# Head-by-head exponential of the query softmax on ScalarE, and a ring of four PSUM banks for the query and value products

## The reference

```python
qkv = jnp.einsum('bnc,cf->bnf', x, w_qkv)
q, k, v = jnp.split(qkv, 3, axis=-1)          # each reshaped to B, N, 8 heads, 64
q = jax.nn.softmax(q, axis=-1)                # over the 64 columns of a head
k = jax.nn.softmax(k, axis=1)                 # over the 1250 nodes
context = jnp.einsum('bnhd,bnhe->bhde', k, v / N)
out = jnp.einsum('bhde,bnhd->bhen', context, q / sqrt(64))
```

## Time and profile before

| | |
|---|---|
| median of 3 runs | 558.52 us (558.47 to 559.47) |
| the profiled execution | 561.2 us |
| its span, first to last instruction | 558.6 us, granted clock 0.954 |
| busy: PE, DVE, ACT, POOL | 496.5, 342.3, 233.5, 165.5 us |
| the changed stage | 105.6 to 182.9 us of the span |

### The profile page before, as it was taken

The page is one execution under the profiler, slowest core; times in us unless marked ns, Lnnn a source line. Parts: engine busy times, 40 slices in busy tenths (PEclk is TensorE's granted clock), DMA queues, the critical chain, the costliest instruction groups (busy, mean ns, idle before and its releaser), DMA issues.

```text
span 558.6 us, 11588 instructions
## 1 busy us (share of the span) xinstructions
PE 496.5 (89%) x3909; PEld 389.9 (70%) x3909; DVE 342.3 (61%) x731; ACT 233.5 (42%) x533; POOL 165.5 (30%) x142
## 2 busy tenths in 40 slices
PE   2988599999889889999999988799999978989792
PEld 2776488766455756679988877599888857856541
DVE  4679888589798267555266543212675375537686
ACT  4744122553323422224255448211355377733343
POOL 1564400040860300024974610000446023304312
PEclk9998799999999899999999997899999957999997
DMA  8502200020200200020000010000210294000014
GB/s 247 164 2 75 76 1 3 1 75 1 77 0 1 78 1 1 1 79 0 0 1 0 11 66 1 3 1 0 82 48 0 79 412 191 2 0 2 0 54 129
DMA packets 5246, 27.45 MB, mean 49 GB/s; under 512 B 1036, under 2 KB 1161, under 8 KB 3544
## 3 DMA queue, kind: packets, MB, share of 16 engines
q1 hardware_dynamic: 5208, 26.92, 13.9%
HBM read 24.36 MB, written 2.56 MB: 48 GB/s over the span
## 4 chain that ended last, share of the span: by engine, by line
PE 65%; DVE 19%; ACT 7%; issue 5%; POOL 1%; DVEq 1%; DMA 1%; ACTq 0%; SPq 0%
PE ps L455 38%; PE ps L600 15%; PE ps L442 4%; PE ps L509 3%; PE ps L499 2%; DVE stage L1447 2%; DVE ohs L1078 1%; DVE r L1159 1%; DVE r L1087 1%; DVE late L1088 1%; PE ps L709 1%; PE ps L439 1%; ACT r L920 1%; DVE r L1517 1%; ACT late L837 1%
## 5 line engine op out<-in xcount | busy, mean ns | idle before, releaser
L455 PE MATMUL ps<-late,wslot 128*128 x960 | 104.7, 269 | 1.0 <-ACT ohs L894 0.9
L455 PE MATMUL ps<-r,wslot 128*128 128x250 f16 x840 | 99.8, 279 | 5.1 <-DVE r L1087 5.0
L455 PEld LDWEIGHTS ps<-late,wslot 128*128 128x128 f16 x960 | 92.3, 97 | 13.1 <-issue 3.5
L1578 POOL TENSOR_TENSOR wslot<-stage,wslot 128x2048 f16<-128x2048 f32 x9 | 36.8, 4086 | 206.4 <-ACT wslot L752 129.0
L455 PEld LDWEIGHTS ps<-r,wslot 128*128 128x128 f16 x840 | 84.3, 101 | 18.5 <-DVE r L1087 6.6
L600 PE MATMUL ps<-late,r 125*128 (+1 forms) x800 | 90.5, 274 | 4.9 <-issue 3.4
L600 PEld LDWEIGHTS ps<-late,r 125*128 125x128 f16 x800 | 78.6, 99 | 15.1 <-issue 6.0
L455 PE MATMUL ps<-wslot,r 128*125 128x512 f16 x300 | 71.3, 387 | 2.6 <-DVE late L1088 2.6
L1088 DVE SCALAR_TENSOR_TENSOR late<-ps,late 128x250 f32 (+2 forms) x60 | 29.1, 502 | 61.2 <-ACT late L927 55.6
L455 PEld LDWEIGHTS ps<-wslot,r 128*125 128x125 f16 (+1 forms) x300 | 39.5, 138 | 26.5 <-DVE late L1088 4.0
L759 ACT ACTIVATE late<-ps 125x500 f16<-125x500 f32 (+1 forms) x25 | 14.7, 588 | 100.6 <-PE ps L442 100.6
(11 more groups left out here) (174 smaller groups left out, 697.2 us busy)
## 6 DMA issues: line engine op xcount, KB each, us to landing
late<-in_tv SPq DMA_DIRECT2D x2, 4096.0 KB, 17.4
x<-in_x SPq DMA_DIRECT2D x5, 448.0 KB
out<-r SPq DMA_DIRECT2D x10, 224.0 KB
stage<-in_w_up SPq DMA_DIRECT2D x2, 1024.0 KB, 5.1
stage<-in_w_down SPq DMA_DIRECT2D x2, 1024.0 KB, 4.9
stage<-in_w_lin SPq DMA_DIRECT2D x1, 1024.0 KB, 6.8
stage<-in_w_k SPq DMA_DIRECT2D x1, 1024.0 KB, 6.1
stage<-in_w_q SPq DMA_DIRECT2D x1, 1024.0 KB, 4.7
```

The lines of the kernel that those rows point to most:

```text
L455: last = nc.tensor.matmul(out, stat_(hs, b), mov(hm, b), start=start and n == 0, stop=stop and n == 3 * blocks - 1)
L1578: nc.gpsimd.tensor_tensor(wslot[:, i % SLOTS, 1].rearrange("p k n -> p (k n)"), stage[:, :], wslot[:, i % SLOTS, 0].rearrange("p k n -> p ...
```

## The change

Three things change in the QV stage. The q and v products get a family of their own, "z", with a ring of four banks (0 to 3) in place of two. The subtraction on VectorE is dropped: VectorE now makes the negated maximum of each head and scales that small tile (125x8), and ScalarE reads the product from PSUM in eight exponentials of 64 columns, each with its own bias column and an accumulated sum, so that the sum reduction on VectorE is dropped too. The bank of a q tile is freed by the last of those exponentials, not by VectorE's subtraction. Nothing of the order of tiles changes.

```diff
-    "n": [("qv", 2 * T, "dve", 0), ("m", KB, "dve", 1), ("mix", T, "dve", 0), ("ffn2", T, "dve", 0)],
+    "z": [("qv", 2 * T, "dve", 0)],
+    "n": [("m", KB, "dve", 1), ("mix", T, "dve", 0), ("ffn2", T, "dve", 0)],
...
-RING = {"n": 2, "t": 4, "x": 2, "y": 2}
+RING = {"z": 4, "n": 2, "t": 4, "x": 2, "y": 2}
...
+            def qv_tile(i):
+                kind, t = QV[i]
+                if i < RING["z"]:
+                    wait_done(pe, "t", "k", 17 + i)
+                else:
+                    last_kind, last_t = QV[i - RING["z"]]
+                    pe.wait_ge(q_exp if last_kind == "q" else v_low, last_t + 1)
+                passes(bank("z", i % RING["z"])[0:P, :], lambda h, b: xn_t[:, h, b, t * P:(t + 1) * P],
+                       lambda h, b: weight(kind)[:, h, b, :], KB).then_inc(full["z"], 1)
...
-                    wait_done(act, "n", "qv", i + 1)
-                    nc.scalar.activation(q_nat[:, t, :], q_nat[:, t, :], ACT.Exp, scale=S_XW).then_inc(q_exp, 1)
+                    act.wait_ge(q_minus, t + 1)
+                    for h in range(H):
+                        part = slice(h * DH, (h + 1) * DH)
+                        last = nc.scalar.activation(q_nat[:, t, part], bank("z", i % 4)[0:P, part], ACT.Exp, scale=S_XW,
+                                                    bias=qmax[:, t, h:h + 1], accum_out=qsum[:, t, h:h + 1])
+                    last.then_inc(q_exp, 1)
...
-                then(nc.vector.tensor_reduce(qmax[:, t, :], q, AX.X, ALU.max))
-                nc.vector.tensor_tensor(heads_of(q_nat[:, t, :]), q, per_head(qmax[:, t, :]), ALU.subtract).then_inc(free["n", "dve"], 1)
+                nc.vector.tensor_reduce(qmax[:, t, :], bank("z", i % 4)[0:P, :].rearrange("p (h d) -> p h d", h=H), AX.X, ALU.max,
+                                        negate=True).then_inc(q_max, 1)
+                dve.wait_ge(q_max, t + 1)
+                nc.vector.tensor_scalar(qmax[:, t, :], qmax[:, t, :], S_XW, None, ALU.mult).then_inc(q_minus, 1)
 
             def q_sum(t):
                 dve.wait_ge(q_exp, t + 1)
-                then(nc.vector.tensor_reduce(qsum[:, t, :], heads_of(q_nat[:, t, :]), AX.X, ALU.add))
                 nc.vector.reciprocal(qsum[:, t, :], qsum[:, t, :]).then_inc(q_rec, 1)
```

More of the change, by code:

```diff
@@ L99 @@
 }
-RING = {"n": 2, "t": 4, "x": 2, "y": 2}
-BANKS_FROM = {"qv": ("t", "k", 17), "agg0": ("n", "mix", 9), "ffn2": ("t", "ffn1", 9)}
+RING = {"z": 4, "n": 2, "t": 4, "x": 2, "y": 2}
+BANKS_FROM = {"agg0": ("n", "mix", 9), "ffn2": ("t", "ffn1", 9)}
 def before(family, phase, who=None, high=False):
@@ L146 @@
 assert sum(WINDOWS.values()) * J == NWIN and J == HT
-READER = {"lin": ("t", "lin"), "k": ("t", "k"), "q": ("n", "qv"), "v": ("n", "qv"), "out": ("n", "m"), "up0": ("t", "up0"),
+READER = {"lin": ("t", "lin"), "k": ("t", "k"), "q": ("z", "qv"), "v": ("z", "qv"), "out": ("n", "m"), "up0": ("t", "up0"),
           "down0": ("t", "down0"), "up1": ("t", "up1"), "down1": ("t", "down1"), "gate": ("t", "gate")}
@@ L168, in bank @@
                 return ps[:, slot, 0:CH]
-            return ps[:, {"n": 0, "x": 4, "y": 6}[family] + slot, :]
+            return ps[:, {"z": 0, "n": 0, "x": 4, "y": 6}[family] + slot, :]
         x = sb("x", [P, T, D])
@@ L475, in transposed, with natural_tile @@
                     product_chunk(phase, w, mov, j, bass.ts(j, CH))
[L477 to L480, removed]
+            def natural_tile(phase, mov, w, t):
+                wait_bank(pe, "n", phase, t, t % 2)
+                passes(bank("n", t % 2)[0:P, :], lambda h, b: mov[:, h, b, t * P:(t + 1) * P], lambda h, b: w[:, h, b, :], KB
                        ).then_inc(full["n"], 1)
+            def qv_tile(i):
[7 more added lines that the diff above has]
+                       lambda h, b: weight(kind)[:, h, b, :], KB).then_inc(full["z"], 1)
             def natural(phase, mov, w, blocks=KB, ready=None, bias=None):
@@ L548, in _ @@
                     wait_weight(pe, "v")
-                natural_tile("qv", xn_t, weight(kind), t, i)
+                qv_tile(i)
                 if kind == "q" and KN_LAG <= t < Q_FIRST:
@@ L556, in _ @@
             windows("v", HT - 1, 1, 2)
-            wait_done(pe, "n", "qv", 2 * T)
+            pe.wait_ge(q_exp, T)
+            pe.wait_ge(v_low, T)
             wait_done(pe, "x", "kn", T)
@@ L845, in _ @@
                             high_tile_nat("x", "kn", k_nat, S_K, u, u % 2)
-                    wait_done(act, "n", "qv", i + 1)
-                    nc.scalar.activation(q_nat[:, t, :], q_nat[:, t, :], ACT.Exp, scale=S_XW).then_inc(q_exp, 1)
-                else:
-                    wait_full(act, "n", "qv", i)
-                    nc.scalar.activation(v_nat[:, 0, t, :], bank("n", i % 2)[0:P, :], ACT.Copy, scale=1 / S_W).then_inc(v_high, 1)
+                    act.wait_ge(q_minus, t + 1)
[4 more added lines that the diff above has]
+                    last.then_inc(q_exp, 1)
+                else:
+                    wait_full(act, "z", "qv", i)
+                    nc.scalar.activation(v_nat[:, 0, t, :], bank("z", i % 4)[0:P, :], ACT.Copy, scale=1 / S_W).then_inc(v_high, 1)
                     windows("v", t // 2, t % 2, 2)
@@ L1266, in _ @@
                     dve.wait_ge(v_high, t + 1)
-                    low(v_nat[:, 1, t, :], bank("n", i % 2)[0:P, :], v_nat[:, 0, t, :], 1 / S_W).then_inc(free["n", "dve"], 1)
+                    low(v_nat[:, 1, t, :], bank("z", i % 4)[0:P, :], v_nat[:, 0, t, :], 1 / S_W).then_inc(v_low, 1)
                     if t == T - Q_FIRST:
```

8 lines of the change are left out of this document (2 added, 6 removed).

## The result

The changed kernel takes 562.29 us in the median of 18 executions (559.22 to 565.94); the kernel before took 559.42 on the same chips (558.11 to 561.3). The ratio is 1.0048, with a 95% interval of 1.003 to 1.0067: slower by some 2.7 us (1.7 to 3.7), where 1.5 were forecast. The sign was right, and the size was not. 562.29 lies 0.3 us above the forecast's range of 558.1 to 562.0. Of the 2.2 us between it and 560.1, 0.9 are the kernel before itself, with 559.42 in 18 executions and 558.52 in the three of the forecast. The profiled execution of the changed kernel took 562.57 us, with a span of 560.7.

A forecast was written before the change was run, and what follows sets the result against it. TensorE, busy 496.5 of 558.6 us, was taken to bound the kernel. +1.9 (first wait for kn2) +0.1 (rounds) -0.4 (v1's bank wait) gave +1.5 to +1.6 us, so 560.1 us, range 558.1 to 562.0.

The forecast's parts named there:

- The price of a head: ScalarE's 64-column exponential with its read: 0.305 us a head, 2.45 us a tile, bounds 2.1 to 2.95 us a tile.
- kn2: TensorE's second pair of key transposes: would start 1.9 us later, behind a wait of near 2.8 us.
- The rounds behind it: After the second pair of key transposes: TensorE 3.47 us a round, ScalarE 3.45, just level; +0.1 us in the sum.
- the bank waits of v1 to v3: TensorE's three waits for a bank, 2.6 us together, would vanish with four banks.
- TensorE's clock: No clock fall behind the new wait was in the sum, since the waits at 117, 142 and 150 us had none.
- rival (a): A second clock fall behind the new wait from 117 to 119.8 us adds 1.7 us, giving 561.8; chance 0.15.
- A half clock near 120 us: Sign that the forecast is wrong: TensorE at half clock behind the wait for the second pair of key transposes.
- rival (b): The clock fall at 182 to 188 us does not come, giving 558.4, no change; chance 0.15.
- The ring: Four banks free v1 of its bank wait: -0.4 us in the sum.
- the other bank waits: Bank waits of v2 and v3: won by TensorE, given back in waits for w2 to w4.
- The payback of VectorE: VectorE from low half to next window: 1.6 us in place of 2.77, paying back 1.2 us a q tile.
- GpSimd's train as what holds w4: GpSimd's ten back-to-back multiplications start 1.55 us later and hold w4; v6 starts near 166.6 us, against 165.10.

The follow-up runs named there:

- e2_wide_exp: The changed kernel with one 512-column exponential a tile in place of eight of 64, softmax left out in part; ratio 0.9976 to the kernel before.
- e1_ring_only: The kernel before with the ring of four banks alone, query softmax as before; ratio 0.9979 to the kernel before.
- The four kernels above: The changed kernel with small multiplication and bias columns (1.0048), bias only (1.0030), multiplication only (0.9971) and neither (0.9934); ratios to the kernel before.
- e5_after_out_early: The changed kernel with the split of the out weight moved ahead of v0's window; ratio 1.0030 to the kernel before.
- e15: The changed kernel with ScalarE's key copies ahead of the exponentials and the small multiplication on ScalarE; ratio 0.9977 to the kernel before.
- e16: The changed kernel without VectorE's small multiplication and without a bias in the exponentials; ratio 0.9934 to the kernel before.
- e18_no_mult_bias: The changed kernel without VectorE's small multiplication, with a constant bias column in each exponential; ratio 1.0030 to the kernel before.
- e19_mult_no_bias: The changed kernel with VectorE's small multiplication kept but no bias in the exponentials; ratio 0.9971 to the kernel before.

## Why the prediction came out as it did

- **The price of a head** held: 0.29 us and not 0.305, 2.32 us a tile and not 2.45, well inside the bounds. What the row of 250 columns could not show is that a third of it is the bias column. The estimate by the Trainium skill, ScalarE: Activation LUTs, section What ACT_TABLE_LOAD costs, 0.24 us before the read and 2.6 us a tile, was above the measured 0.20 and 2.32 us. The advice of 512 elements that the prediction takes from the Trainium skill, VectorE: DVE Perf Modes, section on the TRN2 errata, is given there for sources in SBUF; these exponentials read PSUM, and nothing in the sum rests on it.
- **kn2** held: a wait of 2.65 us where "near 2.8" was named, 1.80 us later than before where 1.9 was worked out. The rounds behind it stay with TensorE at 3.46 us, and the bank waits of v1 to v3 are gone, as forecast.
- **TensorE's clock** is the step that failed: the sum has no term for it, since I argued that the waits at 117, 142 and 150 us had no fall, and gave rival (a) 0.15. A half clock near 120 us was among the signs of being wrong, and it came. Those waits were of 1.7 us or less, and a single execution was no proof that even they are free; the new one is of 2.65 us. The fall came in the profiled execution of the changed kernel and of four of the five others with such a wait, and it was worth 1.6 us (give or take 1.6) when the wait was filled. Over all executions and all places the reduced clock took 2.0 us more (27.7 against 25.5 to 25.8 for the kernel before). The rival's price, 1.7 us, fits, and its chance was too small. The fall of the earlier trace rows did not vanish, as rival (b) had it, but doubled in that execution; a fall between 178 and 190 us stands in ten of the twenty profiled executions, so it was never a fixed part of either kernel.
- **The ring** was probably sized too small: 1.2 us alone (0.3 to 2.1) for the 0.4 that I gave it, which is just inside the interval. I had said that the other bank waits would be given back in the waits for w2 to w4; v6 is 0.72 us earlier with the ring alone.
- **The payback of VectorE** failed. From v1's low half to the window's first instruction I allowed 1.6 us; it took 2.32 us (144.07 to 146.39). That instruction then took 0.98 us in place of 0.38, so w2's one-hot is 3.21 us behind the low half, against 3.07 before. The multiplication took 0.97 us; both lie beside GpSimd's multiplications. v1's low half is 4.7 us later than before, at +41.51 for +36.80, where 3.5 were forecast, and v6 3.6 later: 1.1 us was paid back of the 2.0 forecast. I had named "what the small multiplication waits for GpSimd" and put no number on it. e2_wide_exp is no faster than e1_ring_only, so even with a cheap exponential the relief was worth nothing that could be measured. The four kernels above make it likely that 1 to 2 us of it were there to be had without the multiplication.
- **GpSimd's train as what holds w4** failed as a mechanism. e5_after_out_early started the train 6 us earlier and w4's one-hot came 0.84 us earlier. In the changed kernel VectorE has no idle time from v1's low half to w4's one-hot, so there its own chain holds w4, and ScalarE's late copy of v1 (VectorE idle 5.60 us, not 2.83) moves that whole chain. GpSimd's last multiplication waits for q9's reciprocal in that chain, and it and the scaling fall beside w4's one-hot, which takes 2.40 us in 18 of the twenty profiled executions (1.55 in e15 and e16). In e5_after_out_early the chain is broken by the wait for v3's copy, so what would hold w4 if VectorE were faster is not shown.

With the measured terms the sum is +1.8 for kn2, -1.2 for the ring and +2.0 for the clock, 2.6 us against 2.7 measured. That it closes so well is partly luck: the ring and the clock have an uncertainty of about 1 us each, the clock's is a total over the whole execution, and kn2's place is from one execution. The likely 1.2 us of the heads at q7 to q9 is not in it as a term of its own and may lie in any of them. The forecast's error is the clock, partly set off by the ring.

## What to carry to other kernels

When a change makes a wait of TensorE longer than any in its stage, price it with a fall of the clock behind it (here 1.7 us, nearly the 1.8 us by which the wait grew), and don't take one execution's full clock as proof against it. When a large operation is split into small ones, ask what each piece costs apart from its columns, and price the bias column and the accumulator read each by itself. Relief on an engine counts only after what it then waits for has been priced, and an order of queue in which the critical copies go first can be worth more than the change itself.

## What the runs showed of the hardware that was not expected

- A bias column costs ScalarE 0.10 us in an ACTIVATE of 64 columns (0.20 us to the next instruction in the changed kernel and e18_no_mult_bias, 0.10 in e16_no_mult), as much as everything else in it up to the accumulator read.
- A multiplication of 125x8 in SBUF took 0.17 us alone and 0.69, 0.97, 1.00, 1.74 (e19_mult_no_bias at q2) and 3.45 us beside GpSimd; as tensor_tensor it took 0.17, 0.69 and 0.97; reductions, reciprocals and instructions that read PSUM kept their length. The Trainium skill, SBUF — State Buffer, section SBUF: two separate sides, says that a VectorE operation in a two-port mode or with two operands in SBUF takes a port pair that it shares with GpSimd, and that the later of the two waits for the whole instruction of the other. The trace agrees: GpSimd's split runs from 110.63 to 114.70 in the changed kernel, and VectorE's instruction of 113.73 ends at 114.73. Which mode that instruction ran in, no run shows.
- Products that nobody reads, in place of a wait, made a kernel faster by 1.6 us (give or take 1.6); the clock stayed at 2.4 GHz where it had fallen before.
- The executions of one kernel differ by up to 1.4% (1.2% for the changed one). Over the 218 executions of the changed kernel and the experiments, about half of the spread within a kernel goes with the granted clock (correlation 0.67). Falls of 1.7 us each stand at places that differ from one kernel's profiled execution to the next, also between kernels with the same waits. Two profiled executions can't settle a difference of 2 us; the mean clock of a dozen executions says more, though single kernels still overlap.
